# Stacking the next context's tail in step 11 of the batch in front, and copying it to its place in step 4

## What is computed

```python
# first attention: 16 heads of 64, weights wq, wk, wv, wo
normed = x * rsqrt(mean(x * x) + 1e-6) * norm_w
q, k, v = heads(normed @ wq), heads(ctx @ wk), heads(ctx @ wv)
x = x + merge(softmax(q @ k.T) @ v) @ wo
# second attention: one head, no weights
x = x + softmax(x @ ctx.T) @ ctx
```

## Times and profile before

| | us |
|---|---|
| median of 3 runs | 588.2 (587.67 to 589.69) |
| the profiled execution | 588.1 |
| its span in the profile | 586.4 |
| PE busy | 568.3 (97%) |
| POOL busy | 456.6 (78%) |
| DVE busy | 454.7 (78%) |
| ACT busy | 393.5 (67%) |

### The profile page before, as it was taken

How to read it: one execution, slowest core, us unless ns; L and a number is a source line. 1 busy time by engine, 2 the same in 40 slices (tenths; PEclk the granted TensorE clock), 3 DMA queues, 4 the chain that set the end, 5 groups by cost and what they waited for, 6 DMA issues and landing times.

```text
span 586.4 us, 10901 instructions
## 1 busy us (share of the span) xinstructions
PE 568.3 (97%) x3781; PEld 514.2 (88%) x3781; DVE 454.7 (78%) x641; ACT 393.5 (67%) x517; POOL 456.6 (78%) x532
## 2 busy tenths in 40 slices
PE   7999999999999999999999999999999999999997
PEld 7878888898999889999999899898899888988885
DVE  5778699679886988879886898868887788868504
ACT  5677667758675876757766677757768476756803
POOL 3337785997789887987879897997789977999810
PEclk9999999999999999999999999999999999999999
DMA  7066847766566667666567766666666765656400
GB/s 224 1 161 161 206 128 177 184 173 156 151 176 173 193 155 186 167 189 155 148 175 180 190 169 158 180 186 150 158 176 175 196 163 155 179 146 177 120 1 8
DMA packets 47808, 92.45 MB, mean 158 GB/s; under 512 B 14698, under 2 KB 20234, under 8 KB 47754
## 3 DMA queue, kind: packets, MB, share of 16 engines
q1 hardware_dynamic: 39834, 76.71, 51.9%
q10 hardware_dynamic: 7920, 15.05, 9.5%
HBM read 8.72 MB, written 0.41 MB: 16 GB/s over the span
## 4 chain that ended last, share of the span: by engine, by line
PE 71%; DVE 8%; ACT 5%; POOL 5%; issue 5%; SPq 4%; DMA 1%; ACTq 1%
PE ps_o L1238 30%; PE ps_s L1117 9%; PE ps_s L1121 9%; PE ps_s L1118 9%; DVE neg_max L912 5%; PE ps_m L1161 4%; SPq L469 4%; POOL turned_p L566 3%; PE ps_m L1015 3%; ACT probs L715 2%; PE ps_o L1234 2%; DVE o_norm L886 1%; PE ps_m L1034 1%; ACT o_part L756 1%; DMA x_rows<-in_x_dram 1%
## 5 line engine op out<-in xcount | busy, mean ns | idle before, releaser
L566 POOL TENSOR_TENSOR turned_p<-turned_p 128x1408 fp32r<-128x1408 f32 (+1 forms) x109 | 338.9, 3110 | 10.3 <-ACT turned_p L744 9.4
L715 ACT ACTIVATE probs<-ps_s,neg_max 128x1444 f32<-128x1444 f32 (+1 forms) x109 | 160.0, 1468 | 135.0 <-DVE neg_max L912 129.3
L1238 PE MATMUL ps_o<-turned_p,c_hi 128*128 128x256 f32 (+2 forms) x1273 | 248.8, 291 | 1.7 <-DVE o_norm L886 1.7
L912 DVE TENSOR_REDUCE neg_max<-ps_s 128x1 f32<-128x1444 f32 (+1 forms) x111 | 184.1, 1659 | 64.5 <-PE ps_s L1121 64.0
L1238 PEld LDWEIGHTS ps_o<-turned_p,c_hi 128*128 128x128 f32 x1273 | 206.4, 189 | 3.8 <-issue 3.1
L1238 PE MATMUL ps_o<-turned_p,c_lo 128*128 128x256 f32 (+2 forms) x693 | 185.4, 270 | 0.0
L935 DVE STREAM_TRANSPOSE blocks<-probs 128x1408 f32<-128x1408 f32 (+1 forms) x109 | 178.1, 1634 | 0.8 <-issue 0.6
L744 ACT ACTIVATE turned_p<-turned_p 128x1536 fp32r<-128x1536 f32 (+1 forms) x109 | 156.4, 1435 | 4.6 <-DMA turned_p<-blocks 4.6
L1238 PEld LDWEIGHTS ps_o<-turned_p,c_lo 128*128 128x128 f32 x693 | 131.3, 189 | 0.0
L1117 PE MATMUL ps_s<-cT_hi,q_hi 128*128 128x512 f32 (+3 forms) x312 | 121.4, 389 | 1.1 <-DVE q_lo L813 1.1
L1121 PE MATMUL ps_s<-cT_hi,q_lo 128*128 128x512 f32 (+3 forms) x312 | 118.8, 381 | 0.0
(11 more groups left out here) (150 smaller groups left out, 450.9 us busy)
## 6 DMA issues: line engine op xcount, KB each, us to landing
turned_p<-blocks SPq DMA_DIRECT2D x667, 96.0 KB, 2.2
turned_p<-blocks ACTq DMA_DIRECT2D x141, 96.0 KB, 2.6
ctx_raw<-in_ctx_dram SPq DMA_DIRECT2D x8, 704.0 KB
turned_p<-blocks SPq DMA_DIRECT2D x40, 48.0 KB, 2.0
turned_p<-blocks ACTq DMA_DIRECT2D x24, 48.0 KB, 2.1
wq_sb<-in_L_xattn_wq_dram SPq DMA_DIRECT2D x2, 256.0 KB, 5.4
wk_sb<-in_L_xattn_wk_dram SPq DMA_DIRECT2D x2, 256.0 KB, 5.6
wv_sb<-in_L_xattn_wv_dram SPq DMA_DIRECT2D x1, 512.0 KB, 6.8
```

The costliest lines, as they stand in the source:

```text
L566: pool.tensor_tensor(lo, lo.bitcast(F32), hi.bitcast(F32), ALU.subtract).then_inc(remainder, 1)
L715: act.activation(probs[step % 2][0:m, 0:S], score_tile(step, m), ACT.Exp, bias=neg_max[0:m, s:s + 1], accum_out=sums[0:m, s:s + 1]).then_i ...
L912: dve.tensor_reduce(neg_max[0:m, s:s + 1], score_tile(step, m), AX.X, ALU.max, negate=True).then_inc(maxed, 1)
L1238: t = pe.matmul(*todo[i], start=(i == 0), stop=(i == len(todo) - 1))
```

## The change

GpSimd's five stacking instructions for batch b + 1 are issued in step 11 of batch b, behind the remainder of that step. They no longer write the slot in `c_hi` but leave the stacked tail in `tail_a`, with `result` as a second scratch tile. In step 4 of batch b + 1 a single copy (`place_tail`) puts it in `c_hi`. Batch 0 does both at once at the start. GpSimd now waits in step 11 for the loaded context and, from batch 2 on, for the store of the output two batches back, which reads `result`. DVE waits ahead of its write to `result` (step 4) until the stacking that used it as scratch is over. The counts of `stack_steps` go from 3 to 4 for each batch.

```diff
-    STACK_STEP = 4
+
+    STACK_STEP, PLACE_STEP = 11, 4
@@ SP, ahead of load_ctx(b + 1)
-                    sp.wait_ge(stack_steps, 3 * (b + 1))
+                    sp.wait_ge(stack_steps, 4 * (b + 1))
@@ GpSimd
             def stack_tail(b):
-                raw = ctx_raw[:, FULL, :]
-                dst = c_hi[b % 2][:, FULL, :]
+                raw, low = ctx_raw[:, FULL, :], result[:, :]
                 pool.tensor_copy(tail_a[:, :].bitcast(F32R), raw).then_inc(stack_steps, 1)
-                pool.wait_ge(stack_steps, 3 * b + 1)
-                pool.tensor_tensor(dst, raw, tail_a[:, :], ALU.subtract).then_inc(stack_steps, 1)
-                pool.wait_ge(stack_steps, 3 * b + 2)
+                pool.wait_ge(stack_steps, 4 * b + 1)
+                pool.tensor_tensor(low.bitcast(F32R), raw, tail_a[:, :], ALU.subtract).then_inc(stack_steps, 1)
+                pool.wait_ge(stack_steps, 4 * b + 2)
                 pool.tensor_scalar(tail_a[:, :], tail_a[:, :], hi_rows[:, 0:1], None, ALU.mult)\
                     .then_inc(tail_masked, 1)
-                pool.tensor_scalar(dst, dst.bitcast(F32), lo_rows[:, 0:1], None, ALU.mult)\
-                    .then_inc(tail_masked, 1)
+                pool.tensor_scalar(low, low, lo_rows[:, 0:1], None, ALU.mult).then_inc(tail_masked, 1)
                 pool.wait_ge(tail_masked, 2 * (b + 1))
-                pool.tensor_tensor(dst, tail_a[:, :], dst.bitcast(F32), ALU.add)\
-                    .then_inc(stack_steps, 1)
+                pool.tensor_tensor(tail_a[:, :], tail_a[:, :], low, ALU.add).then_inc(stack_steps, 1)
+
+            def place_tail(b):
+                pool.wait_ge(stack_steps, 4 * b + 3)
+                pool.tensor_copy(c_hi[b % 2][:, FULL, :], tail_a[:, :]).then_inc(stack_steps, 1)
...
                 take_remainder(*group_at(step, LO_LAG))
-                if s == STACK_STEP and 1 <= b < B:
+                if s == STACK_STEP and b + 1 < B:
+                    pool.wait_ge(ctx_loaded, 64 * (b + 2))
+                    if b >= 2:
+
+                        pool.wait_ge(stored, 16 * (b - 1))
+                    stack_tail(b + 1)
+                if s == PLACE_STEP and 1 <= b < B:
                     if b >= 2:
                         pool.wait_ge(product, unit_no(("late", b - 2, ODD)))
-                    pool.wait_ge(ctx_loaded, 64 * (b + 1))
-                    stack_tail(b)
+                    place_tail(b)
@@ DVE, ahead of its write to result
                         dve.wait_ge(late_inverted, bb + 1)
+                        dve.wait_ge(tail_masked, 2 * min(bb + 3, B))
+                        dve.wait_ge(stack_steps, 4 * min(bb + 3, B) - 1)
@@ PE, ahead of the first products of a batch
-                        pe.wait_ge(stack_steps, 3 * (bb + 1))
+                        pe.wait_ge(stack_steps, 4 * (bb + 1))
```

More of the change, by code:

```diff
@@ L524, in stack_tail @@
             def stack_tail(b):
-                raw = ctx_raw[:, FULL, :]
-                dst = c_hi[b % 2][:, FULL, :]
+                raw, low = ctx_raw[:, FULL, :], result[:, :]
                 pool.tensor_copy(tail_a[:, :].bitcast(F32R), raw).then_inc(stack_steps, 1)
-                pool.wait_ge(stack_steps, 3 * b + 1)
-                pool.tensor_tensor(dst, raw, tail_a[:, :], ALU.subtract).then_inc(stack_steps, 1)
-                pool.wait_ge(stack_steps, 3 * b + 2)
+                pool.wait_ge(stack_steps, 4 * b + 1)
+                pool.tensor_tensor(low.bitcast(F32R), raw, tail_a[:, :], ALU.subtract).then_inc(stack_steps, 1)
+                pool.wait_ge(stack_steps, 4 * b + 2)
                 pool.tensor_scalar(tail_a[:, :], tail_a[:, :], hi_rows[:, 0:1], None, ALU.mult)\
                     .then_inc(tail_masked, 1)
-                pool.tensor_scalar(dst, dst.bitcast(F32), lo_rows[:, 0:1], None, ALU.mult)\
-                    .then_inc(tail_masked, 1)
+                pool.tensor_scalar(low, low, lo_rows[:, 0:1], None, ALU.mult).then_inc(tail_masked, 1)
                 pool.wait_ge(tail_masked, 2 * (b + 1))
-                pool.tensor_tensor(dst, tail_a[:, :], dst.bitcast(F32), ALU.add)\
-                    .then_inc(stack_steps, 1)
+                pool.tensor_tensor(tail_a[:, :], tail_a[:, :], low, ALU.add).then_inc(stack_steps, 1)
+            def place_tail(b):
+                pool.wait_ge(stack_steps, 4 * b + 3)
+                pool.tensor_copy(c_hi[b % 2][:, FULL, :], tail_a[:, :]).then_inc(stack_steps, 1)
             pool.wait_ge(ctx_loaded, 16 * 4)
             stack_tail(0)
+            place_tail(0)
             def split_tail(step):
```

## The result

The changed kernel takes 597.95 us (median of 5 executions, 595.80 to 598.73) against 588.86 of the kernel before (5 executions, 587.67 to 590.29): a ratio of 1.014, 95% interval 1.0115 to 1.0166. That is 9.1 us by the medians, 8.2 by the ratio; 594.1 had been forecast, 6.0 above the profiled execution. The direction is right; the size is 2 to 3 us more than forecast.

A forecast was written before the change was run, and what follows sets the result against it. PE, busy 97% of the span, was taken as the bound, so GpSimd's work counts only where PE waits for it. 2.29 + 4.92 - 1.25 = +5.96 us on 588.1 gave 594.1 us, range 590.5 to 597.5.

The forecast's parts named there:

- batch 0, step 13: PE's first product of step 13, already waiting for GpSimd, comes late by the whole stack: +2.61 us.
- batch 0, by step 15: Time PE had already lost to GpSimd at step 15's start comes back: -0.32 us, leaving batch 0 at +2.29.
- batch 1, projection and product: Around step 7, earlier tails let the projection start 0.99 sooner and end the product's 0.26 wait: -1.25 us.
- batches 1, 3, 5, step 13: Stack less GpSimd's 0.61 idle ahead of the tails delays step 13's first product: +0.62 us each.
- batches 2, 4, step 13: No GpSimd idle time to absorb the stack, so step 13's first product comes +1.33 us late in each.
- batch 6, step 13: First product delayed by the stack, but PE already stood 0.86 for DVE: +0.40 us.
- The gain in batches 2 to 7: Step 7's gap hangs on ACT and DVE, so earlier tails gain nothing; bound 2.0 us over six batches.
- step 7 of batches 2 to 7 gets shorter: One of three signs that would show the forecast wrong; no gain was counted there.
- The added waits: New GpSimd waits in step 11 and DVE waits in step 4 cost zero; DVE's could cost up to 1.2 us.
- Given back: Rival: step 13's lateness is absorbed by PE's wait in step 15, leaving batch 1's gain: 586.9 us, chance 0.09.
- Tails too late: Rival: step 11's tails reach DVE late in step 12, about 0.5 more in seven batches: 597.6 us, chance 0.10.
- Shorter stack: Rival: with scratch destinations the masks run like the copy, each stack 0.68 us shorter: 589.8 us, chance 0.06.

The follow-up runs named there:

- e2: Kernel before, but batch 1's stack alone made in step 11 of batch 0 and placed in step 4; the others stay in step 4: 591.63 us, ratio 1.0038.
- e3: Changed kernel plus 24 small PE matmuls in the idle time of batch 0's step 13, ahead of the products: 596.92 us, ratio 1.0123.
- e7: The kernel of e3 without a further edit, timed again on the same chip as e6: 595.44 us, ratio 1.0117.
- e6: Changed kernel without an edit, run again for a second profile: 596.85 us, ratio 1.0148 against the kernel before.
- e1: Changed kernel, but batch 1's stack stays in step 4 ahead of its place copy; the other six are in step 11: 593.56 us, ratio 1.0074.
- e4: Changed kernel with the stack in step 12 instead of step 11: 588.59 us, ratio 1.0024 against the kernel before.
- e5: Changed kernel with the stack in step 2 of its own batch, place copy still in step 4: 585.96 us, ratio 0.9966 against the kernel before.
- e8: Changed kernel with the stack in step 10 instead of step 11: 587.27 us, ratio 0.9995 against the kernel before.

## Why the prediction was right, and where it was too small

The mechanism held: the stack delays the remainder of step 12, GpSimd releases step 13 in all seven batches, and nothing behind gives that back. The sum, term by term, in us; "measured" is the difference of PE's starts between the profile after and the second one of before:

| term | forecast | measured |
|---|---|---|
| batch 0, step 13 | +2.61 | +2.63 |
| batch 0, by step 15 | -0.32 | +1.51 |
| batch 1, projection and product | -1.25 | -1.27 (0.95 + 0.32) |
| batches 1, 3, 5, step 13 | 3 x 0.62 | 0.79, 0.62, 0.63 |
| batches 2, 4, step 13 | 2 x 1.33 | 1.14, 1.11 |
| batch 6, step 13 | +0.40 | +1.21 (and 0.34 of chance) |
| sum | +5.96 | +8.37 |

With the 0.34 of chance in batch 6 and the 1.45 of chance at the end this is, to some hundredths, the 10.1 by which the spans differ (596.4 less 586.3). The medians of the two kernels, 9.1 apart by difference and 8.2 by ratio, lie beside the 8.4.

**The step that failed: batch 0.** I wrote that the time lost to GpSimd at step 15, 0.32, "comes back", and carried nothing else from step 13 on. Both were wrong. The start at 85.11 in the earlier trace rows was late for GpSimd by 0.15 of idle time only; in the second profile of before and in the kernel after, DVE's normalisation releases it, 8.57 us behind step 13 at full clock in either profile of before, so there was nothing to give back. And I costed the 3.3 us of idle time as idle time alone. Behind it the granted clock was at its lower level, 1.2 GHz, and that cost 1.51. The two errors make 1.83 of the 2.41 us between 5.96 and 8.37. e2 shows the whole term by itself, e3 and e7 take the clock away from it. The Trainium skill, "TensorE: Matmul & The Clock Gate", Part 1, says that TensorE's clock falls to half when the engine has not been busy, and returns with activity. This trace agrees: 0.43 in place of 0.24 for two products behind the stop, and full speed again at 84.14. The Trainium skill would have led me to ask what the stop does to the clock, and I didn't ask it.

**The second: batch 6.** The forecast was worked out by the right formula from rows of an execution with a chance wait. By the second profile of before it gives 476.05 + 3.22 + 2.61 + 0.05 - 480.62 = +1.31, as in batches 2 and 4. PE's lateness grows there by 1.30, from 7.41 at the product of step 11 to 8.71, and batch 6 had gained 0.09 on the way, which makes the 1.21 of the table. (The whole growth from step 13 of batch 5 is 1.55; 0.34 of it arose in step 15 of batch 5, where the first product waits 0.54 for DVE's normalisation in that profile and 0.20 in the second one of before, and I count it as chance: the same stretch takes 10.28 and 10.34 from step 13 to 15 in after and e6, but 9.43 and 9.45 in e3 and e7, which differ from them only in batch 0.) The 0.86 for DVE in the earlier trace rows doesn't recur at that place. The remainder meant is this one, GpSimd's timeline in the second profile of before (answers to the earlier trace rows):

```profile
476.05 3.22 POOL L566 TENSOR_TENSOR turned_p<-turned_p 128x1408 fp32r<-128x1408 f32 x1
```

**The third: a gain in the even batches.** Batches 2 and 4 lost 0.2 less each than forecast. The formula itself was right: at the product of step 13 PE's lateness grows by 1.30 and 1.28, where 1.33 had been forecast. But it had shrunk by 0.16 and 0.17 before, between step 13 of the odd batch and step 11 of the even one (3.66 to 3.50, and 5.42 to 5.25). About half of that arises in step 7. GpSimd's remainder of step 6 and PE's first product of step 7, batch 2, before:

```profile
181.71 3.17 POOL L566 TENSOR_TENSOR turned_p<-turned_p 128x1408 fp32r<-128x1408 f32 x1
...
184.94 0.39 PE L1234 MATMUL ps_o<-turned_p,rinv_ones 128*128 128x256 f32 x1
```

and after:

```profile
183.94 3.18 POOL L569 TENSOR_TENSOR turned_p<-turned_p 128x1408 fp32r<-128x1408 f32 x1
...
188.48 0.36 PE L1244 MATMUL ps_o<-turned_p,rinv_ones 128*128 128x256 f32 x1
```

Before, the product starts 0.06 behind the end of the remainder, and 3.64 behind the start of the projection (181.30): it waits for GpSimd, although no idle time is printed, because the projection's modelled end lies over it. After, the remainder has ended 1.36 before the product starts, and the product follows the projection (184.91) by 3.57. e2 is the control: its batch 2 has the stack in step 4, and the product again starts 0.05 behind the remainder and 3.72 behind the projection. e1, e4, e5 and e8, which have it elsewhere, show 3.56 or 3.57. The rest of the 0.16 is spread over steps 3 to 9 and stays open.

**Smaller: batch 1** lost 0.17 more than forecast in this profile. In e6, the same kernel, it is 33.04 from the projection to step 13 (116.29 to 149.33), in this one 33.23, and in before 32.76: by e6 the loss is 0.28 + 0.32 = 0.60, e1, e3 and e7 give 0.60, 0.55 and 0.58, and the 0.17 is chance.

**The gain of batch 1** came as worked out: DVE no longer waits for the tails, ACT's part is late next, and the projection stands 0.16 behind the normalisation. The gain in batches 2 to 7 had been costed at nothing, with 2.0 as its bound. That was right for the odd batches; the even ones gained 0.16, 0.17 and 0.09, so that the sign "step 7 of batches 2 to 7 gets shorter", under which I said I would be wrong, did come in them, by 0.07 to 0.09 each. The added waits were rightly costed at nothing: none shows in the rows around step 4 or ahead of the stack.

**The rivals.** *Given back* fell: the gap in step 15 stays at 0.16 while step 13 is 2.63 late, and from the projection of batch 1 on the lateness grows, but for the 0.1 to 0.2 of the even batches, which come from step 4 and not from PE's wait. *Tails too late* had its mechanism once, where it was placed. The timeline of DVE in the kernel after, batch 0:

```profile
76.77 0.30 DVE L949 STREAM_TRANSPOSE blocks<-tails 64x128 f32<-64x128 f32 x1 [0.54 <-POOL tails L560]
```

0.54, where about 0.5 had been worked out; but PE was held up longer by the remainder, so it cost nothing, and the waits of DVE name the tails nowhere else. That the result is near this rival's 597.6 says nothing for it. *Shorter stack* fell: the masks take 0.60 each in the new place, with scratch tiles as destinations, and the two-input subtraction 0.46. By the Trainium skill ("GPSIMD Engine Reference", section 4.1) one-input operations run at about line rate, and two-input ones about twice as slow as on VectorE. In these rows it doesn't hold for the masks: with one tile in, they take 0.60 where the copy takes 0.28.

**The range,** 590.5 to 597.5, had nothing in it for the clock. The forecast was made against a median of 588.2, and with the ratio of 1.014 this gives 596.4, inside; the median of 597.95 itself, beside one of 588.86, lies 0.45 over its upper end. It held by the room left for other mishaps, not by having the right one in it.

## What to carry to other kernels

An instruction moved on an engine that is busy 78% of the time isn't free or dear by that share, but by the idle time between its new place and the wait that reads what stands behind it: moved out of step 4, the same seven stacks of 2.6 us cost 8 to 9 us in step 11, about 1 in step 12, nothing in step 10, and gained about 2 in step 2. When a stop of TensorE grows, ask what the granted clock does behind it: in the profiles, the stops of 2.7 and 3.3 us brought 1.3 and 1.5 us more, while stops of 1.2 to 1.5 us (batches 2, 4 and 6 here, batch 0 in e4) left the clock full. And take two profiles of the kernel before a term is read from one row: a wait of 0.86 and a landing 0.8 us early were both chance. A wait can also hide behind the modelled end of the matmul in front: compare the start of a product with the end of what it reads.

## What the runs showed of the hardware

The granted clock fell at a single stop of 3.3 us in the middle of dense work, some 0.6 us behind its end, and stayed at the lower level for some 3.6 us; the cost was 1.5. At the stop of 2.7 in e6 the first product behind it was slow already, and the cost was 1.26. 24 small matmuls in the stop kept the clock up, in e3 and in e7; in e3 0.54 us of idle time was left behind them.

The same half clock also comes by chance in stretches where PE has short gaps: at the end of the profiles of after and of e7, not of e6, and near the start of those of e3, e5, e6 and e7 (granted clock 0.90 from 8 to 25, against 1.00 in both profiles of before, in after, e1, e2, e4 and e8). It belongs to no edit, since after and e6 are one kernel. At the end it cost 1.45. Near the start it went with a first product of the first group at 50.8 to 51.6, against 49.2 to 50.0 in the others. A term of that size can't be read from one execution of this kernel.
